# Padded weight rows and paced dispatch scatters in a mixture-of-experts block

## The reference, cut to what matters

```
diag = (q * k).sum(d) / sqrt(128); probs = softmax(diag, axis=group)
attn = probs * vsum                       # vsum: v summed over the tokens of a group
scores = softmax(xn @ gate_w + gate_b); top 2 of 16 experts, weights = their scores
routed = sum over the 2: w * ((silu(xn@w1+b1) * (xn@w3+b3)) @ w2 + b2)      # inner width 176
shared = silu(xn@sw1+sb1) * (xn@sw3+sb3) @ sw2 + sb2                        # inner width 352
out = x + attn + routed + shared
```

## Time and profile before

| | us |
|---|---|
| median of 3 runs | 291.55 (291.29 to 292.16) |
| the profiled execution's own time | 292.58 |
| its span, from the first to the last instruction | 290.8 |
| PE busy | 217.7 (75%) |
| DVE busy | 188.0 (65%) |
| POOL busy | 156.6 (54%) |
| POOL's 64 scatters, line 384 | 68.1 |
| mean granted clock of TensorE | 0.891 |

### The profile page before, as it was taken

One profiled execution on the slowest core, in us unless ns is written; L12 is line 12 of the kernel. 1 busy time (PEld: TensorE's weight loads), 2 busy tenths in 40 slices (PEclk: granted clock), 3 DMA queues, 4 the chain that ended last, 5 costly groups with the idle time before them and its releaser, 6 DMA issues.

```text
span 290.8 us, 5484 instructions
## 1 busy us (share of the span) xinstructions
PE 217.7 (75%) x1323; PEld 177.7 (61%) x1325; DVE 188.0 (65%) x518; ACT 115.0 (40%) x329; POOL 156.6 (54%) x170
## 2 busy tenths in 40 slices
PE   0679959599499000599989999999999999995000
PEld 0569723597147000257389999999898998994000
DVE  4998885498969105446476666666666666662386
ACT  2134246930043100032316666666565665662000
POOL 6323005777788777772003666666666666666000
PEclk9999998689799655599999999999999999999555
DMA  6999591222111124112300333333333333311698
GB/s 187 314 304 300 148 378 77 86 74 85 75 66 65 74 101 170 61 63 77 75 0 26 101 100 104 91 104 96 88 103 99 93 96 95 96 55 47 203 365 308
DMA packets 35394, 36.74 MB, mean 126 GB/s; under 512 B 5493, under 2 KB 30566, under 8 KB 35030
## 3 DMA queue, kind: packets, MB, share of 16 engines
q1 hardware_dynamic: 28498, 24.54, 28.4%
q0 software_dynamic: 4576, 9.91, 10.1%
q10 hardware_dynamic: 2304, 2.10, 2.1%
HBM read 18.67 MB, written 17.86 MB: 126 GB/s over the span
## 4 chain that ended last, share of the span: by engine, by line
PE 58%; another core or an unknown queue 15%; DVE 11%; DMA 7%; ACT 3%; SPq 3%; issue 1%; POOL 0%; POOLq 0%; DVEq 0%
PE PS L897 13%; PE PS L916 12%; PE PS L894 4%; PE PS L773 4%; PE PS L793 4%; PE PS L814 4%; PE PS L906 3%; PE PS L794 3%; DMA xnT<-ydram 3%; PE PS L890 3%; PE PS L907 3%; SPq L322 3%; DMA gate<-vdram 2%; DVE st L405 2%; PE PS L766 2%
## 5 line engine op out<-in xcount | busy, mean ns | idle before, releaser
L392 POOL DMA_INDIRECT ydram<-fw x79 | 75.9, 960 | 59.1 <-issue 33.3
L384 POOL DMA_INDIRECT xslot<-XR,idx x64 | 68.1, 1064 | 39.8 <-DVE idx L513 20.6
L916 PE MATMUL PS<-fw 89*128 (+1 forms) x316 | 48.7, 276 | 0.1
L629 DVE TENSOR_TENSOR prod<-prod,PS 128x176 f32<-128x176 f32 x79 | 26.7, 338 | 32.2 <-ACT prod L741 32.2
L793 PE MATMUL PS<-xnT,sw 128*128 (+3 forms) x36 | 21.8, 690 | 28.3 <-DVE sS L529 28.3
L916 PEld LDWEIGHTS PS<-fw 89*128 89x128 f32 (+1 forms) x316 | 41.4, 190 | 0.7 <-issue 0.3
L741 ACT ACTIVATE prod<-PS 128x176 f32<-128x176 f32 x79 | 25.1, 318 | 29.8 <-PE PS L897 29.5
L700 ACT ACTIVATE sS<-PS,sbc 128x512 f32<-128x512 f32 (+1 forms) x18 | 12.2, 686 | 61.8 <-PE PS L794 61.7
L897 PE MATMUL PS<-w13h,rxh 128*128 x79 | 34.9, 442 | 0.8 <-DVE rxl L624 0.8
L746 ACT ACTIVATE fw<-PS 88x256 f32<-88x256 f32 x79 | 30.0, 380 | 0.9 <-PE PS L907 0.6
L793 PEld LDWEIGHTS PS<-xnT,sw 128*128 128x128 f32 (+1 forms) x36 | 6.3, 202 | 38.3 <-DVE sS L529 33.8
(11 more groups left out here) (123 smaller groups left out, 372.0 us busy)
## 6 DMA issues: line engine op xcount, KB each, us to landing
fw<-xslot SPq DMA_DIRECT2D x79, 72.0 KB, 1.9
xslot<-fw SPq DMA_DIRECT2D x6, 864.0 KB, 8.8
fw<-in_w SPq DMA_DIRECT2D x1, 2816.0 KB, 9.5
X<-in_x SPq DMA_DIRECT2D x4, 512.0 KB, 6.2
XR<-ydram SPq DMA_DIRECT2D x8, 256.0 KB, 5.5
xnT<-ydram SPq DMA_DIRECT2D x8, 256.0 KB, 8.0
out<-X ACTq DMA_DIRECT2D x16, 128.0 KB, 5.7
fw<-in_w SPq DMA_DIRECT2D x1, 1424.0 KB
```

The lines of the kernel that those rows point to most:

```text
L384: pool.indirect_dma_start(xslot, bass.IndirectOffsetOnAxis(ap=idx[:, k, t:t + 1], axis=0), XR[:, t, :], None).then_inc(d_sc[k][h], 16)
L392: pool.indirect_dma_start(ydram, bass.IndirectOffsetOnAxis(ap=RX[:, v, P:P + 1].bitcast(I32), axis=0), yb[:, v, :], None).then_inc(d_y[v], 16)
L629: dve.tensor_tensor(ra[:, b, :], sg[:, b, :], PS[:, 2 + b, F:F2], ALU.mult).then_inc(r_a, 1)
L916: ins = pe.matmul(PS[:, 6 + b, 0:P], raT[0:n, b, k * P:(k + 1) * P], w2[0:n, bass.ds(e * 2 * P + k * P, P)], start=(k == 0), stop=(k == 1))
```

## The change

The rows of two arrays are padded with zeros, in DRAM and in the SBUF tiles: `w2` from 89 to 96 rows and the third part of `sw2` from 97 to 112. The matmuls read the same rows as before. And 27 of the 64 dispatch scatters get a wait ahead of them, for a count of PE's steps: 18 for `s_up`, 3 for `s_y`, 6 for `s_z`. The scatters are numbered n = 0 to 63 in the order of POOL's queue.

```diff
+FP = 96
+SP3 = 112
+PACE_UP = {13: 3, 17: 6, 28: 7, 29: 8, 31: 9, 32: 10, 33: 11, 35: 12, 40: 13, 41: 14, 43: 15, 44: 16, 45: 17, 47: 18,
+           52: 19, 54: 20, 55: 21, 56: 22}
+PACE_Y = {18: 2, 22: 4, 26: 8}
+PACE_Z = {20: 1, 24: 2, 37: 3, 39: 4, 49: 5, 51: 6}
-        w2 = fw[0:FH + 1, NE * F2:NE * (F2 + 2 * P)]
+        w2 = fw[0:FP, NE * F2:NE * (F2 + 2 * P)]
-            sp.dma_start(sw2[0:97, 2, :], d["sw2"][256:SF + 1, :]).then_inc(l_sh, 16)
+            sp.dma_start(sw2[0:SP3, 2, :], d["sw2"][256:256 + SP3, :]).then_inc(l_sh, 16)
                     for t in range(half.start, half.stop):
+                        n = k * NT + t
+                        if n in PACE_UP:
+                            pool.wait_ge(s_up, PACE_UP[n])
+                        if n in PACE_Y:
+                            pool.wait_ge(s_y, PACE_Y[n])
+                        if n in PACE_Z:
+                            pool.wait_ge(s_z, PACE_Z[n])
                         pool.indirect_dma_start(xslot, bass.IndirectOffsetOnAxis(ap=idx[:, k, t:t + 1], axis=0),
                                                 XR[:, t, :], None).then_inc(d_sc[k][h], 16)
...
-    w2 = np.zeros((FH + 1, NE, 2, P), np.float32)
+    w2 = np.zeros((FP, NE, 2, P), np.float32)
...
+    sw2 = np.zeros((256 + SP3, P), np.float32)
+    sw2[0:SF] = a[f + "sw2"]
+    sw2[SF] = a[f + "sb2"]
```

More of the change, by code:

```diff
@@ L958, in arrays_of @@
         "biases": b13.reshape(P, NBIAS // P),
-        "sw1": a[f + "sw1"], "sw3": a[f + "sw3"], "sw2": np.concatenate([a[f + "sw2"], a[f + "sb2"].reshape(1, P)], axis=0),
+        "sw1": a[f + "sw1"], "sw3": a[f + "sw3"], "sw2": sw2,
         "sb_a": np.stack([a[f + "sb1"][:256].reshape(2, P).T, a[f + "sb3"][:256].reshape(2, P).T], axis=2),
@@ L962, in arrays_of @@
         "w13": w13.transpose(1, 0, 2).reshape(P, NE * F2),
-        "w2": w2.reshape(FH + 1, NE * 2 * P),
+        "w2": w2.reshape(FP, NE * 2 * P),
     }
```

## The result

The changed kernel took 280.44 us (median of 4 runs, 279.89 to 281.18) against 291.42 us of the kernel before on the same chip (290.91 to 292.16). The ratio is 0.962, with a 95% interval of 0.959 to 0.966: 11.0 us faster, where 9.3 us were forecast. The profiled execution had 279.89 us with a span of 278.1.

A forecast was written before the change was run, and what follows sets the result against it. The dense stage was the longer branch, held by `w2`'s load on one DMA engine. Of 16.5 us won there, 11.1 reach the routed stage, less 1.8 for the clock: 9.3 off 291.55 gives 282.3 us, range 278.8 to 285.0.

The forecast's parts named there:

- the waits' 2.3 us: POOL's dispatch scatters: waits bind at n = 44 and 56, moving n = 63 from 132.50 to 134.8, 2.3 us later.
- the prediction's own sign: POOL's last dispatch scatter: the forecast is wrong if n = 63 starts before 133 or after 136.5 us.
- first rival: Start of routed stage: waits don't bind, or clock holds; both 278.1 us, one of them some 280; chance 0.18.
- The stuck write: SP's queue: 8 KB `vdram` write stuck 67.7 us behind `w2`, whose 89 rows use one DMA engine; padding frees it.
- The shift of the dense stage, 16.5 us: DVE's attention starts at 95.75 in place of 112.24; dense stage ends at 134.0 in place of 150.5 us.
- The lag: POOL's binding waits: a scatter starts 0.81 us after the step it waits for ends, read on line 392.
- What is late next: After the dense stage: POOL's scatters become the later branch by 5.2 us, PE's first table transpose at 139.2.
- The clock, 1.8 us: Routed stage: PE's clock falls in its 5.2 us gap before it, costing 1.8 us, bounds 0 and 2.7.
- The sum: Whole kernel: 11.1 us won at the routed stage's start less 1.8 for the clock, 9.3 us earlier, 282.3 us.
- The second rival: SP's queue: padding does not free it, the waits bind for real, n = 63 at 151.3; 298.7 us, slower; chance 0.04.
- The third: POOL's scatters: each of 27 waits costs even when satisfied; at 0.5 us each the time is 293.5; chance 0.03.

The follow-up runs named there:

- the 20 matmuls: Changed kernel plus 20 matmuls with unused results ahead of PE's routed stage, against the kernel before (375.96 us on that chip): 332.90 us, ratio 0.884.

## Why the prediction was right

The direction, the size within the stated range and the mechanism of the gain were right. One term, the waits' 2.3 us, was wrong, and by the prediction's own sign: n = 63 started before 133. What came true is the branch of its first rival in which the waits don't bind and the clock falls ("some 280"; chance of the rival 0.18), not the main forecast within 1.3 us.

**The stuck write.** Right, and shown by the number of rows: `vdram` lands at 50.9 with 96 rows, is out of the way at 76.8 with 94 and at 112.5 with 97, and `w2`'s padding alone carries the gain. With the slow load issued behind it, `Vb` was fetched at 60.02; what that order is worth in time on the first kind was not measured.

**The shift of the dense stage, 16.5 us.** Right for the mechanism; its size depends on the execution. Without waits the attention started at 95.58 and the dense stage ended at 133.5, as forecast. In the changed kernel's profile it started at 91.37. That goes with the clock: in 44 to 50 us and 56 to 62 us PE had 0.82 and 0.68 in the profile of before and 1.00 and 1.00 in this one. It is no effect of the change: the kernel with `sw2` padded alone had 1.00 in both windows too, with `w2` at 89 rows, and the one with both paddings and no waits had 0.83 and 0.70. I read one execution as if its clock were the kernel's.

**The waits bind and cost 2.3 us.** This is the step that failed: they cost nothing. The forecast had step 22 at 125.1 and let n = 56 go at 125.9. In the profile after step 22 ended at 120.50, and n = 56 stood at 123.79 behind the scatters ahead of it; no other scatter was held either. The reason is the 4.6 us by which the dense stage was ahead of the forecast (129.4 in place of 134.0), which goes with the clock as above. The lag was also too long, 0.44 to 0.48 us in place of 0.81, but with 0.81 nothing would have bound in this profile either. The working itself held: with the steps at their old times n = 63 was forecast at 151.3 and measured at 149.98. In an execution as late as that without waits, step 22 ends at 124.5 and n = 56 would be held to 124.9, against 123.5 that it had: an estimate of 1.5 us. None of the three profiles of the changed kernel shows one; in the latest of them step 22 ended at 122.26, and n = 56 started at 123.66.

**What is late next.** Right: POOL's scatters. The first rival's start of 136.9 was the true one (136.96), since n = 63 stayed where it was.

**The clock, 1.8 us.** Right in size, though no run changed the clock alone. The routed stage, from PE's first transpose to the start of POOL's last scatter, took 117.1 us before, and 118.1, 119.3, 118.8, 118.5 and 119.3 in five profiles with `w2` padded: 1.0 to 2.2 us more, 1.7 in the mean. PE's time at a clock of 0.50 in the stage was 3.9, 6.1, 5.1, 3.4 and 5.9 us in the same order, and with waits alone 3.4 us, with 0.8 us more. So the loss is by and large the greater the longer the slow time, and a quarter to some 0.4 of it. The Trainium skill (TensorE: Matmul & The Clock Gate, "HAM oscillation") would make it half of the slow time. By that rule an estimate for the 3.9 us of the profile after is 2.0 us; the stage lost 1.0 there, so that the trace shows less than the rule.

**The sum.** Forecast 11.1 - 1.8 = 9.3. Measured in the five profiles: PE's first transpose came 13.5 us sooner in the mean, and 13.5 - 1.7 = 11.8. Between medians it was 11.0, for the profiled execution of before, on which 13.5 rests, was 1.2 us above its median. The 2.5 us by which 11.8 exceeds the forecast are the waits' term, 2.3, and rounding.

**The second rival.** It was tried as the waits alone: 297.08 measured, 298.7 worked out. n = 63 was 1.3 us earlier than worked out, 0.9 of it because step 22 ended at 140.69 and not at 141.6, and 0.4 by the shorter lag. PE's first transpose was 1.4 us earlier, and the clock's term was 0.8 in that profile (117.9 against 117.1) and not 1.8. The rival did not name the wait that held longest, that of n = 43 for step 15. **The third** (a satisfied wait costs) falls: n = 63 stands at 132.3 without the 27 waits and at 132.5 to 132.9 with them.

## What to carry to other kernels

The number of rows of the loads tried here set how many DMA engines they got; with 89 and 97 rows it was one, and an 8 KB write issued behind them on that queue landed only after the whole of them. Look for it as one sixteenth of the engines busy for a long time and a tiny transfer that takes tens of us to land; pad the rows, which was worth 11 us here, or issue it last, whose worth was not shown. When the longer branch is cut, put the other branch's end beside it first: of 17 to 23 us won in the dense stage some 13.5 reached the next stage. Check a releaser that a profile names against the count that the instruction waits for: here PE was named for scatters whose step had ended 4 us before. And a wait whose event has come cost nothing here, but one execution's clock is no ground for saying which of two events comes first: the dense stage ended anywhere from 127.9 to 133.5 in five profiles of padded kernels.

## What the runs showed of the hardware

Chips of one type are not alike: the same kernel before took 292 us on some and 376 on others. On those PE and DVE stalled while GpSimd's indirect scatters were in flight, so that PE came to the routed stage at 199.5 to 204.0 us in place of 150.3, and the routed stage took some 30 us longer. The waits, which are neutral elsewhere beside the padding, saved 45 us there (376.08 to 331.20). The padding, which saved 11 us elsewhere, showed nothing beside them (0.880 without, 0.884 with it and the 20 matmuls). In the kernel after, the time from PE's end to the fall of its clock was 2.6 us in the gap at 90.5 and 4.7 us in the gap at 129.4. A load of 89 or 97 rows of 16 KB went through one DMA engine at 0.70 us a row, and one of 94 rows through two.
